# Gates, normalisation and router of the second image pair placed between the expert matmuls of images 0 and 1, on one PSUM bank of their own

## What is computed

```
x = x + conv_layer(groupnorm(x))                       # 7x7 tap softmax, not touched by the change
t = tokens(x)                                          # 4 images, 3136 tokens, 64 channels
n = layernorm(t)
attn = softmax(a_i + b_j + (n*wc) n^T) n               # not touched
z, r, f = tanh / sigmoid / sigmoid of [n, attn] @ w.T + b
t = t + r * n + f * z                                  # the "gates"
n = layernorm(t)                                       # normalisation
g = n @ Wg + bg;  top 2 of 8 experts, softmax over the two      # the "router"
t = t + sum_e w[:, e] * (gelu(n @ W1[e] + b1[e]) @ W2[e] + b2[e])    # the experts, hidden width 256
```

## Time and profile before

| | |
|---|---|
| median of 3 runs | 2011.94 us |
| the profiled execution, its own time | 2013.85 us |
| its span in the trace | 2012.1 us |
| mean granted TensorE clock | 0.96 of full speed |
| busy: PE, DVE, ACT, POOL | 86%, 61%, 58%, 33% |
| gates_and_experts | from 1457.8 us to the end, 554 us |
| of it before the first expert matmul | 1457.8 to 1552.4 us |

### The profile page before, as it was taken

The page is one execution under the profiler, slowest core; times in us unless marked ns, Lnnn a source line. Parts: engine busy times, 40 slices in busy tenths (PEclk is TensorE's granted clock), DMA queues, the critical chain, the costliest instruction groups (busy, mean ns, idle before and its releaser), DMA issues. The chain is left out here.

```text
span 2012.1 us, 32023 instructions
## 1 busy us (share of the span) xinstructions
PE 1724.3 (86%) x11589; PEld 609.7 (30%) x11589; DVE 1227.3 (61%) x1736; ACT 1165.7 (58%) x1565; POOL 660.0 (33%) x378
## 2 busy tenths in 40 slices
PE   5468787877765799999999999999885979999998
PEld 1011111111102333333333333333243423333333
DVE  3249999899986766655655566555256444333343
ACT  3799999899723544444444444444354655656664
POOL 0798888888551300000000000000122312222222
PEclk9799999999986899999999999999997989999999
DMA  2220210120132110000000000100011002000000
GB/s 95 84 104 36 81 61 32 71 74 30 61 128 82 33 40 14 14 11 14 14 12 15 15 14 15 45 12 14 19 75 32 1 0 48 8 7 10 7 10 9
DMA packets 25161, 72.89 MB, mean 36 GB/s; under 512 B 5456, under 2 KB 14672, under 8 KB 23632
## 3 DMA queue, kind: packets, MB, share of 16 engines
q1 hardware_dynamic: 24896, 70.28, 10.9%
q10 hardware_dynamic: 144, 0.96, 0.1%
HBM read 47.84 MB, written 13.62 MB: 31 GB/s over the span
## 5 line engine op out<-in xcount | busy, mean ns | idle before, releaser
L1088 ACT ACTIVATE at_prob<-at_ps_s 128x896 f32<-128x896 f32 x336 | 305.9, 917 | 406.7 <-PE at_ps_s L970 406.2
L1257 DVE TENSOR_REDUCE at_mpart<-at_ps_m 128x1 f32<-128x448 f32 (+1 forms) x700 | 399.8, 619 | 194.2 <-PE at_ps_m L959 193.8
L424 DVE TENSOR_TENSOR cm_prod<-cm_ps_ev,win 128x1792 f32<-128x1792 f32 x196 | 388.7, 2018 | 17.5 <-ACT cm_ps_ev L475 9.5
L368 POOL TENSOR_TENSOR cm_diff<-front 128x1792 f32<-128x1792 f32 x98 | 320.7, 3276 | 71.3 <-POOLq L113 38.3
L1710 ACT ACTIVATE ge_hid<-ge_ps,ffn 128x448 f32<-128x448 f32 x448 | 249.6, 634 | 153.7 <-PE ge_ps L1583 153.1
L986 PE MATMUL at_ps_a<-at_prob,win 128*64 128x448 f32 x1344 | 296.4, 554 | 10.1 <-DVE attn L1239 10.1
L581 PE MATMUL cm_ps_acc<-cm_prod,cst 128*32 128x504 f32 x1568 | 221.5, 637 | 76.0 <-DVE cm_prod L424 45.8
L970 PE MATMUL at_ps_s<-vh,front 128*128 (+3 forms) x700 | 248.4, 355 | 1.6 <-DMA vh<-at_mrow 1.6
L970 PE MATMUL at_ps_s<-vl,front 128*128 (+3 forms) x700 | 247.9, 354 | 0.0
L959 PE MATMUL at_ps_m<-front,vh 128*128 128x448 f16 (+1 forms) x700 | 239.8, 357 | 7.7 <-DVE at_mpart L1257 6.9
L895 POOL TENSOR_TENSOR attn<-attn 64x448 f32<-64x448 f32 x28 | 31.6, 1129 | 526.9 <-DMA attn<-attn 526.9
(11 more groups left out here) (205 smaller groups left out, 1775.4 us busy)
## 6 DMA issues: line engine op xcount, KB each, us to landing
win<-x_dram SPq DMA_DIRECT2D x28, 868.0 KB
at_rden<-rden_dram SPq DMA_DIRECT2D x28, 224.0 KB, 3.3
x_dram<-win SPq DMA_DIRECT2D x4, 962.0 KB
conv_out<-cm_cout SPq DMA_DIRECT2D x28, 112.0 KB, 3.5
win<-x SPq DMA_DIRECT2D x2, 1568.0 KB, 12.5
t_dram<-front SPq DMA_DIRECT2D x2, 1568.0 KB, 6.8
front<-attn SPq DMA_DIRECT2D x8, 392.0 KB, 6.2
attn<-attn SPq DMA_DIRECT2D x28, 112.0 KB, 2.2
```

What stands on the lines that cost most here:

```text
L368: pool.tensor_tensor(diff[:, s % ND, 0:n, :].rearrange("p n (r c) -> p n r c", c=W), a.rearrange("p n (r c) -> p n r c", c=W), b, ALU.subt ...
L424: v.tensor_tensor(prod[:, hs, :, 0:CH].rearrange("p s (r c) -> p s r c", c=W), ev.rearrange("p s (r c) -> p s r c", c=W), wv, ALU.mult).th ...
L1088: act.activation(prob_of(s)[0:w, 0:a, :], ps_s[0:w, (s + 1 - par) % 2, 0:a, 0:CH], ACT.Exp).then_inc(exp_done, 1)
L1257: v.tensor_reduce(mpart[0:w, a, kb:kb + 1], ps_m[0:w, e % RB, 0:CH], AX.X, ALU.max).then_inc(rough_max, 1)
```

## The change

The loop of the front now makes gates for 9 chunks (`PLAIN`): seven of pair 0 and two of pair 1, whose tanh results lie in the `part` and `total` tiles. Its groups run one chunk later (`TURN_D` 3, `BACK_D` 6) and `gate_sums` of a chunk's last gate no longer waits for the next chunk. The casts to fp16 are made group by group out of PSUM (ACT `hi`, DVE `lower`), and PE's next `turn_back` waits for them, as all use bank 4.

The router's exponential becomes `Tanh` with scale 0.5. `turn_weights` of pair 0 goes into units 0 and 1. The first unit waits for the first half of the stacked fp16 data only, and no longer for the router's weights.

The other 5 chunks' gates (15 gate sums) go into units 2 to 6, pair 1's turns into units 7 and 8, turns back into 9, logits into 10, its router into 10 to 12 and its `turn_weights` into 12 to 14. All of that goes through PSUM bank 3 (`side`), so in images 0 and 1 `outer` has bank 2 alone and waits for the part of the step before. `hidden` has four banks from the first unit and PE goes in fours throughout. Pair 1's split into fp16 halves moves to POOL (`halves`). Image 1's units are written out too (`units`).

The diff, cut to its core:

```diff
-        WIDE_AT = 5
-        TURN_D, BACK_D = 2, 5
+        HALF = 4 * GROUP * TT
+        EARLY, SECOND_AT = 2, 7
+        PLAIN = NCH + EARLY
+        TURN_D, BACK_D = 3, 6
+        FRONT = NG + BACK_D + 1
...
-
-        def narrow(b, k):
-
-            return b == 0 and k < WIDE_AT
-
-        def hidden_banks(b, k):
-
-            return (0, 1) if narrow(b, k) else (0, 1, 6, 7)
-
-        def hidden_bank(b, k, j):
-            return hidden_banks(b, k)[j % len(hidden_banks(b, k))]
+        side = ps[:, 3]
+
+        def mixed(b, k):
+
+            return b < 2 or (b == 2 and isinstance(k, int))
+
+        def out_bank(b, k, ep):
+
+            return ps_o[:, 0 if b < 2 else ep % 2, :]
...
+        def gate_bank(n):
+
+            return ps[:, n % 4] if n < 3 * PLAIN else side
...
+        def hidden_bank(j):
+            return ps[:, (0, 1, 6, 7)[j % HP2]]
+
+        def group_bank(t, g):
+
+            return ps_n[:, g % 2] if t == 0 else side
 
         def back_bank(t, g):
 
-            return ps[:, 4] if t == 0 else ps_n[:, 0]
+            return ps[:, 4] if t == 0 else side
 
         def logit_bank(t):
 
-            return ps[:, 5] if t == 0 else ps_n[:, 1]
+            return ps[:, 5] if t == 0 else side
 
...
                 def gate_input(n):
                     (t, k), j = divmod(n // 3, NCH), n % 3
-                    if n >= 4:
+                    if n > 3 * PLAIN:
+                        pe.wait_ge(tanh_done, n)
+                    elif n == 3 * PLAIN:
+                        pe.wait_ge(w_out, NG)
+                    elif n >= 4 and n < 3 * PLAIN:
                         pe.wait_ge(tanh_done, n - 3)
                     for i in range(2):
                         part = slice(64 * i, 64 * i + 64)
...
 
                     at, n = tokens_of(g)
                     pe.wait_ge(used, t * NCH + min(NCH, -(-(at + n) // CH)))
-                    if g >= 2:
-                        pe.wait_ge(turned_out, t * NG + g - 1)
-                    elif t > 0:
-                        pe.wait_ge(w_out, t * NG)
+                    if t > 0:
+                        pe.wait_ge(tanh_done, 3 * NB)
+                        if g > 0:
+                            pe.wait_ge(turned_out, NG + g)
+                    elif g >= 2:
...
-                for i in range(NB):
-                    for n in range(3 * i, 3 * i + 3):
-                        gate_input(n)
-                        if n >= 1:
-                            gate_sums(n - 1)
-                    if i == NB - 1:
-                        gate_sums(3 * NB - 1)
+                for i in range(FRONT):
+                    if i < PLAIN:
+                        for n in range(3 * i, 3 * i + 3):
+                            gate_input(n)
+                            if n > 3 * i:
+                                gate_sums(n - 1)
+                        gate_sums(3 * i + 2)
...
+                def aside(u, p):
+
+                    if u < 2 and p % 2 == 0 and 4 * u + p // 2 < NG:
+                        turn_weights(0, 4 * u + p // 2)
+                    if 2 <= u < SECOND_AT and p in (1, 3, 5):
+                        n = 3 * (PLAIN + u - 2) + p // 2
+                        gate_input(n)
+                        gate_sums(n)
+                    if u in (SECOND_AT, SECOND_AT + 1) and p % 2 == 0 and 4 * (u - SECOND_AT) + p // 2 < NG:
+                        turn(1, 4 * (u - SECOND_AT) + p // 2)
+                    if u == SECOND_AT + 2 and p != 6:
+                        turn_back(1, min(p, NG - 1))
+                    if u == SECOND_AT + 3 and p < NG:
+                        logits(1, p)
+                    for at, g in W_TURNS:
+                        if (u, p) == at:
+                            turn_weights(1, g)
+
...
+
+                def outer(j, b, k, u, before):
                     ep = j // HP2
                     n, a, h = order(ep)[j % HP2]
-                    if j % HP2 == 0 and (before or ep >= 2):
+                    if j % HP2 == 0 and mixed(b, k) and (b < 2 or ep == 0):
+                        if before or ep >= 1:
+                            pe.wait_ge(part_done, u * EP + ep)
+                    elif j % HP2 == 0 and mixed(b, k) and ep == 1:
+                        pe.wait_ge(part_done, u * EP)
+                        pe.wait_ge(w_out, 2 * NG)
+                    elif j % HP2 == 0:
                         pe.wait_ge(part_done, u * EP + ep - 1)
                     pe.wait_ge(gelu_done, u * HT + j + 1)
-                    ins = pe.matmul(ps_o[64 * a:64 * a + 64, ep % 2, 0:CH], mat("w2", n, C), hid[:, j % NHB, :],
+                    ins = pe.matmul(out_bank(b, k, ep)[64 * a:64 * a + 64, 0:CH], mat("w2", n, C), hid[:, j % NHB, :],
                                     start=(h == 0), stop=(h == 1), tile_position=(0, 64 * a))
                     if j % HP2 == HP2 - 1:
                         ins.then_inc(o_done, 1)
...
-                    if b % 2 == 0 and isinstance(k, int) and k == 0:
-                        pe.wait_ge(stacked[b // 2], 64)
-                    if b == 0 and k in (0, WIDE_AT):
-                        pe.wait_ge(w_out, NG if k == 0 else 2 * NG)
-                    size = 2 if narrow(b, k) else HP2
-                    for first in range(0, HT, size):
-                        group = range(first, first + size)
+                    if b == 0 and k in (0, 4):
+                        pe.wait_ge(stacked[0][k // 4], 64)
+                    if b == 2 and isinstance(k, int):
+                        pe.wait_ge(stacked[1][0], 64)
+                        pe.wait_ge(stacked[1][1], 64)
+                    for ep in range(EP):
+                        group = range(ep * HP2, ep * HP2 + HP2)
                         for j in group:
                             hidden(j)
...
+                        if mixed(b, k):
+                            aside(u, 2 * ep)
...
-
-                def first_half(t):
-                    act.wait_ge(back_out, (t + 1) * NG)
-                    act.copy(hi[t], xhat[:, t, :]).then_inc(hi_done, 1)
-
-                def weight_exp(t):
+                    if t == 0:
+                        act.copy(hi[t][:, at:at + n], back_bank(t, g)[:, 0:n]).then_inc(hi_done, 1)
+
+                def share(t):
+
                     act.wait_ge(diff_done, t + 1)
-                    act.activation(best[:, 2, :], best[:, 1, :], ACT.Exp).then_inc(exp_done, 1)
+                    act.activation(best[:, 2, :], best[:, 1, :], ACT.Tanh, scale=0.5).then_inc(share_done, 1)
...
+                def lower(g):
+
+                    at, n = tokens_of(g)
+                    v.wait_ge(hi_done, g + 1)
+                    v.tensor_tensor(lo[0][:, at:at + n], back_bank(0, g)[:, 0:n], hi[0][:, at:at + n],
+                                    ALU.subtract).then_inc(split, 1)
...
+                def halves(g):
+
+                    at, n = tokens_of(g)
+                    pool.wait_ge(back_out, NG + g + 1)
+                    pool.tensor_copy(hi[1][:, at:at + n], xhat[:, 1, at:at + n]).then_inc(hi_done, 1)
+                    pool.wait_ge(hi_done, NG + g + 1)
+                    pool.tensor_tensor(lo[1][:, at:at + n], xhat[:, 1, at:at + n], hi[1][:, at:at + n],
+                                       ALU.subtract).then_inc(split, 1)
+
```

More of the change, by code:

```diff
@@ L1396, in gates_and_experts @@
         sent = sem("ge_sent")
+        W_TURNS = [((SECOND_AT + 5 + (g + 2) // 4, 2 * ((g + 2) % 4)), g) for g in range(NG)]
         def mat(name, i=0, n=128):
@@ L1473, in gate_sums @@
                         other = slice(64 - 64 * i, 128 - 64 * i)
-                        ins = pe.matmul(ps[part, n % 4, 0:CH], wa[other, j * C:(j + 1) * C],
+                        ins = pe.matmul(gate_bank(n)[part, 0:CH], wa[other, j * C:(j + 1) * C],
                                         attn[other, 2 * t + 1, columns_of(k)], start=False, stop=True,
@@ L1494, in turn_back @@
                     pe.wait_ge(normed, t * NG + g + 1)
-                    if g >= 1:
+                    if g >= 1 and t == 0:
+                        pe.wait_ge(split, g)
+                    elif g >= 1:
                         pe.wait_ge(back_out, t * NG + g)
+                    elif t > 0:
+                        pe.wait_ge(turned_out, 2 * NG)
                     for n in group_tiles(g):
@@ L1555, in outer @@
-                def outer(j, u, before):
+                def aside(u, p):
[14 more added lines that the diff above has]
+                            turn_weights(1, g)
@@ L1594, in body @@
+                    if b == 2 and isinstance(k, int):
[3 more added lines that the diff above has]
+                        group = range(ep * HP2, ep * HP2 + HP2)
                         for j in group:
                             hidden(j)
[L1596 to L1598 removed]
+                        if mixed(b, k):
+                            aside(u, 2 * ep)
+                        if ep > 0:
+                            weights(b, k, u, ep - 1)
```

(43 more changed lines are left out.)

285 lines of the change are left out of this document (145 added, 140 removed).

## The result

| | before | after | predicted |
|---|---|---|---|
| median | 2012.68 us (4 runs, 2011.4 to 2014.27) | 1991.01 us (4 runs, 1990.67 to 1992.84) | 1990.4 (1983 to 2004) |
| ratio, 95% interval | | 0.9894 [0.9877, 0.9911] | 0.989 |
| the profiled execution: its time, span | 2013.85, 2012.1 | 1991.12, 1989.3 | |
| the stage, from its first DVE row to the end | 554.3 | 534.8 | 532.8 |

What follows compares the result with a forecast made beforehand. It took PE to set the pace in the units, with idle time before and inside the first ones to win. 34.0 + 8.8 - 21.3 = 21.5 us off the median of 2011.94 gave 1990.4 us, range 1983 to 2004.

Steps and rivals of the forecast that it cites:

- Mark 1: First copy of spread weights (L1859) in unit 2: predicted at 1561.2 us, 34.0 us earlier than before.
- the cycle through one bank: End of the front: turn back, two ACT copies, DVE's `lower` and handovers take 2.6 us a group, nearly four groups left.
- The router's 9.9 us: Router of pair 0, between logits done at 1509.4 and weights ready at 1519.5: 9.9 us, against 17.9 before.
- Units 0 and 1: From weights ready to unit 2's first copy: 36.1 us of PE work, 3.0 for low clock, 2.6 waiting for DVE residuals.
- Mark 2: First copy of spread weights in unit 7: 98.2 us after unit 2's, at 1659.4 us, 42.8 us earlier than before.
- the gate: One gate standing alone between steps on PE in units 2 to 6: 1.8 us, between 0.75 and 2.5, counted 14 times.
- Mark 3: First copy of spread weights in unit 14: 21.3 us added to the old 102.2 from unit 7's, at 1782.9, 21.5 earlier.
- the 2.2 us for DVE behind POOL: Between the first copies of units 7 and 14: DVE waits behind POOL's split of pair 1, 2.2 us, possibly nothing to 9.
- Rival 1: Side work costs PE more: waits of 0.1 to 0.3 us at 56 steps, or 2.5 us gates; 1996 to 2006; chance 0.25.
- Rival 2: Output bank becomes the bound at 56 steps of images 0 and 1: 0.8 us waiting a step gives 2035; chance 0.05.
- rival 3: ACT table switches, two 1.28 us loads at 15 gates and one tanh: some 30 us lost, 2020; chance 0.02.
- Rival 4: One-bank cycle or router chain much longer than summed, units start 15 to 20 us later: 2006 to 2010; chance 0.05.

Runs made afterwards that it cites:

- e9: The changed kernel, unaltered, run again in a later session: 1992.43 us, ratio 0.9896 to the kernel before.
- e4: The changed kernel with one output bank for images 2 and 3 too, each step waiting for the part of the step before: 1992.86 us, ratio 0.9899.
- e2: The kernel before with only the router's exponential replaced by tanh: 2010.31 us, ratio 0.9989.
- e11: The changed kernel with hidden blocks in groups of two in units 0 to 4 alone: 2001.04 us, ratio 0.994.
- e5: The changed kernel with hidden blocks in groups of two again in all units of images 0 and 1: 2013.69 us, ratio 1.0011.
- e6: The changed kernel with groups 4 and 6 of pair 0 turned back through bank 2 instead of bank 4: 1990.95 us, ratio 0.9896.

## Why the prediction was right

**The sum.** It said 21.5 us off; the medians say 21.7 (2012.68 - 1991.01), the stage lengths 19.5 to 20.5. That the median was met within 1 us is in part luck: in two other sessions it is 19.3 and 21.4 us off, and 3.3 us of the first difference lie ahead of the stage. In the stage, three errors of 2.6, 3.7 and -4.1 us cancel to 2.

**Mark 1**, said 103.4 us from the start, came at 106.0, 105.2 and 104.9. The step that was short is the cycle through one bank, 2.6 us a group. It is 3.07: PE's own part, the turn back, was taken at its full-clock 0.50 us and takes 0.89 (1500.65 - 1499.77), since the granted clock from 1500 to 1520 us is 0.50. That is 0.39 of the missing 0.47, and nearly four cycles, as the forecast counts them, make 1.8 of the 2.2 us by which the first hidden matmul is late (53.8 us into the stage, where 51.6 was said). The router's 9.9 us are exact. DVE's timeline, first and last row:

```profile
1508.42 0.63 DVE L1835 TENSOR_TENSOR ge_lg<-ge_ps,ffn 128x384 f32<-128x384 f32 x2 [1.56 <-PE ge_ps L1559]
...
1509.69 0.57 DVE L1849 TENSOR_TENSOR ge_eq<-ge_lg,ge_best 128x400 f32<-128x400 f32 x1
...
1517.71 0.57 DVE L1869 TENSOR_TENSOR ge_lg<-ge_one,ge_eq 128x400 f32<-128x400 f32 x1
```

The comparison that took 5.62 us beside POOL takes 0.57 with POOL idle. Units 0 and 1 took 42.1 us (1560.47 - 1518.35) where 41.7 was said, with one wait of 2.4 for DVE's first weights where 2.6 was given to residuals. Over the matmuls' 36.1 and this wait stand 3.6 us, 2.4 in e9, where 3.0 was given to the low clock.

**Mark 2**, said 98.2 us later, came 101.9 later. The step that failed is in part bookkeeping: two turns of pair 1 in unit 7 stand ahead of the mark and were counted behind it, 2.0 us. The other part is the gate, 1.93 and not 1.8 us, 14 times: 1.8 us. No wait is left between the marks.

**Mark 3**, said 123.5 us later, came 119.4 later. Over the old 102.2 that is 17.2 us, and with the two turns that stand ahead of the mark 19.2. The matmuls and the 0.9 of waiting at unit 12 had been summed to 19.1; the wait is 1.0. What was too high is the 2.2 us for DVE behind POOL. That contention is there, on DVE's timeline and POOL's beside it:

```profile
1740.32 0.57 DVE L1854 TENSOR_TENSOR ge_one<-ge_eq,ge_best 128x400 f32<-128x400 f32 x1
1740.92 1.40 DVE L1855 SCALAR_TENSOR_TENSOR ge_lg<-ge_one,ge_lg 128x400 f32<-128x400 f32 x1
```

```profile
1740.48 1.40 POOL L2011 TENSOR_TENSOR ge_total<-ge_part 128x448 f32<-128x448 f32 x1 [5.41 <-DVE ge_part L1954]
```

An operation of 0.58 us, started while POOL's sum ran, ends 0.4 us after the sum's end (1742.32 and 1741.88), as the one in the earlier trace rows did (1532.78 and 1532.35). The Trainium skill ("SBUF — State Buffer", section "🔬 SBUF: two separate sides") says that a DVE operation with two SBUF inputs waits for a GpSimd operation that reads SBUF and started first, until it is finished; this row and the earlier trace rows agree. From 1740 to 1752 us it lengthens four DVE operations by 2.8 us in all. In PE's waits it shows as the 0.4 us once, and perhaps in part of the 1.0 at unit 12, since a step has about 3 us of room on DVE.

**The rivals.** Rival 1, waits at each step: the two lists of waits show 1.4 us in 220, so it is out, and a gate costs 0.13 of waiting. It is true in kind, since a gate does cost more than the matmuls' 1.8, but by 0.13 and not 0.7 us. Rival 2 fell with e4, rival 3 with e2. Rival 4 is true in kind, the bank's cycle being 0.47 us a group longer, but at 2 us and not 15 to 20.

**What the forecast did not see.** It read mark 2's old 107 us as pair 1's steps, a narrow `hidden` and its router, and gave the grouping no price. e11 shows one: with twos in the five units where the kernel before had them, 10.7 of the stage's 20 us are lost. Of these 5.2 are shape changes (five units at 1.03) and 4.3 waits at the start, as in e5. So that the side work has a bank of its own, and PE can go in fours, is a good part of the gain. How much the grouping gives by itself, with the gates left in the front, was not tried.

## What to carry to other kernels

Work that an engine did under another's wait costs its full price once it is moved into a stretch where that engine sets the pace; sum both sides, and count for the moved work its changes of matmul shape, not its columns alone. Before fine work on banks, look at how PE's list is grouped: matmuls of one shape in long rows cost nothing extra, and rows half as long cost a quarter of a microsecond a step here. Compare stages by marks of their own, since untouched stages ahead shifted by 4 us from run to run.

## What was not expected of the hardware

- A change of matmul shape costs time on both sides: 0.09 us from a 128x128 fp16 to a 128x64 fp32 matmul and 0.10 to 0.13 back. A slot of four 64x64 matmuls takes 0.90 us alone and 0.75 in a row of its kind, and in the front of the kernel before, the sums of another gate run beside it in the same 0.75.
- Tanh and Gelu follow each other without a table load, at 15 tanhs of the gates that stand between Gelus, and a load that there is holds ACT for its 1.28 us only.
- At the end of the front the turn back at 1496.70, behind a wait of 1.8 us, is the first at half speed (1.09 us, where the one at 1493.15 takes 0.62). From there, where PE waits 0.46 us at each group, the granted clock is 0.50, the level of 1.2 GHz, and it stays there through the router (PE busy for 12.2 of 20 us). A turn back takes 0.89 us and the logits of a group 1.57, against 0.50 and 0.81 at full clock. So PE became the next bound of a chain in which it had only waited (e6).
